# Attention values stored unturned and divided when they are reloaded, copies moved in SP's list, row blocks first in a key block

## The reference

```python
xn = layernorm(x)
q, k, v = xn @ Wq.T, xn @ Wk.T, xn @ Wv.T        # 16 query heads, 8 key heads, 16 numbers each
energy = q . k + alibi                            # alibi: -|i - j| * 2^-(head + 1)
att = softmax(energy / 4) @ v                     # two query heads share a key head
attention = att @ Wo.T + bo
scale = max(abs(xn)) / 127, per token
linear = (round(xn / scale) as int8 @ weight_q.T) * scale * weight_scale + bias
out = x + attention + linear
```

## Time and profile before

| | |
|---|---|
| median of three runs | 1607.19 us (1605.15 to 1607.93) |
| profiled execution, its span | 1606.43 us, 1604.5 us |
| PE busy | 1507.3 us, 94% |
| DVE busy | 1394.1 us, 87% |
| ACT busy | 1183.8 us, 74% |
| POOL busy | 1073.4 us, 67% |
| granted TensorE clock, mean | 0.978 |
| chain that ended last | PE 53%, DVE 31%, issue 8%, SP 4%, DMA 3% |

### The profile page before, as it was taken

One profiled execution on the slowest core, in us unless ns is written; L12 is line 12 of the kernel. 1 busy time (PEld: TensorE's weight loads), 2 busy tenths in 40 slices (PEclk: granted clock), 3 DMA queues, 4 the chain that ended last, 5 costly groups with the idle time before them and its releaser, 6 DMA issues.

```text
span 1604.5 us, 42517 instructions
## 1 busy us (share of the span) xinstructions
PE 1507.3 (94%) x16284; PEld 584.2 (36%) x16284; DVE 1394.1 (87%) x1698; ACT 1183.8 (74%) x2331; POOL 1073.4 (67%) x1627
## 2 busy tenths in 40 slices
PE   5789989999899998999989999899998999899999
PEld 5323323333333333333333334333333333233333
DVE  6889989999799997999979999799987988899991
ACT  3467777777687775887757887677776777688885
POOL 6457877777688875787757787577785776433332
PEclk9899999999999999999999999999999999999999
DMA  6423233343324333333333333333333332212211
GB/s 169 130 62 84 71 99 79 89 98 84 105 72 106 96 79 98 93 93 101 84 84 95 103 90 90 89 94 97 94 86 85 95 85 69 80 44 70 70 42 61
DMA packets 197291, 140.98 MB, mean 88 GB/s; under 512 B 107040, under 2 KB 165728, under 8 KB 197088
## 3 DMA queue, kind: packets, MB, share of 16 engines
q1 hardware_dynamic: 197088, 138.27, 33.0%
HBM read 81.40 MB, written 35.63 MB: 73 GB/s over the span
## 4 chain that ended last, share of the span: by engine, by line
PE 53%; DVE 31%; issue 8%; SPq 4%; DMA 3%; POOL 0%; ACT 0%; POOLq 0%; ACTq 0%
DVE row_max L999 29%; PE ps_ring L1279 17%; PE ps_pv L1355 15%; PE ps_row L1296 11%; PE ps_ring L1395 4%; PE ps_ring L1415 3%; DMA q_again<-q 2%; PE ps_ring L1398 1%; DVE pv_turned L1039 1%; PE ps_row L1279 1%; PE ps_ring L1409 1%; SPq L497 1%; PE ps_row L1387 1%; SPq L464 0%; DMA base<-x 0%
## 5 line engine op out<-in xcount | busy, mean ns | idle before, releaser
L999 DVE TENSOR_REDUCE row_max<-ps_row 128x1 f32<-128x1024 f32 x1024 | 1199.2, 1213 | 153.8 <-PE ps_row L1298 138.5
L1171 ACT ACTIVATE probs<-ps_ring 128x512 f32<-128x512 f32 x2048 | 1083.7, 601 | 284.8 <-PE ps_ring L1279 282.3
L1279 PE MATMUL ps_ring<-q,k 122*32 122x512 bf16 x8192 | 639.2, 385 | 5.6 <-DMA q<-neg_max_t 4.7
L762 POOL TENSOR_TENSOR probs<-probs,near 128x256 f32<-128x256 f32 x512 | 374.2, 731 | 368.5 <-ACT probs L1171 362.8
L1355 PE MATMUL ps_pv<-probs,v_unit 128*32 128x512 f32 x4096 | 537.9, 601 | 0.0
L1279 PEld LDWEIGHTS ps_ring<-q,k 122*32 122x32 bf16 x8192 | 216.5, 95 | 511.7 <-ACT probs L1171 324.6
L1296 PE MATMUL ps_row<-k,q 64*128 64x512 bf16 x944 | 329.7, 390 | 68.1 <-DMA q_again<-q 43.2
L1298 PE MATMUL ps_row<-k_again,q_again 64*128 64x512 bf16 x944 | 329.6, 390 | 0.0
L1296 PEld LDWEIGHTS ps_row<-k,q 64*128 64x128 bf16 x944 | 83.9, 93 | 362.9 <-issue 197.8
L1355 PEld LDWEIGHTS ps_pv<-probs,v_unit 128*32 128x32 f32 x4096 | 125.2, 110 | 55.1 <-issue 9.1
L1298 PEld LDWEIGHTS ps_row<-k_again,q_again 64*128 64x128 bf16 x944 | 83.8, 93 | 0.0
(11 more groups left out here) (84 smaller groups left out, 1009.1 us busy)
## 6 DMA issues: line engine op xcount, KB each, us to landing
parts_dram<-parts SPq DMA_DIRECT2D x59, 288.0 KB, 3.3
q_again<-q SPq DMA_DIRECT2D x63, 256.0 KB, 3.4
token_b<-token_dram SPq DMA_DIRECT2D x53, 256.0 KB, 4.0
q<-parts_dram SPq DMA_DIRECT2D x128, 96.0 KB
k<-parts_dram SPq DMA_DIRECT2D x256, 32.0 KB
q<-parts_dram SPq DMA_DIRECT2D x128, 64.0 KB
att_dram<-att_unit SPq DMA_DIRECT2D x126, 64.0 KB
att_t<-att_dram SPq DMA_DIRECT2D x56, 128.0 KB, 2.9
```

What stands on the lines that cost most here:

```text
L762: pool.tensor_tensor(here, here, near[:, u % KV_HEADS, :].rearrange("p (e n) -> p e n", e=GROUP), ALU.mult).then_inc(weighted, 1)
L999: dve.tensor_reduce(row_max[:, par, e, qb:qb + 1], ps_row[qb % 2][:, :], AX_X, ALU.max, negate=True).then_inc(row_max_found, 1)
L1171: act.activation(probs[:, c % PBUFS, e, h * HALF:(h + 1) * HALF], ring_bank(u, c, e, h), ACT.Exp, scale=SCALE).then_inc(ring_freed, 1)
L1279: mm = pe.matmul(to[at, :], weights[:, at], moving, start=start, stop=stop)
```

## The change

1. **Values unturned.** DVE's two transposes, its reciprocal of the turned sums and the multiplication by it (on DVE or POOL) go, but for the last unit. ACT copies `ps_pv` to `att_raw` after the exponentials of c = 1 (`keep_pv`). SP stores all 128 rows (`store_att`), reads the rows of sums back as 128 by 16 (`load_sums`), DVE takes the reciprocal before the fourteenth reduction of the unit (`find_rsum`, in c = 6), and SP stores it (`store_rsum`). When a pair of tiles is loaded, its reciprocals come along, each row repeated 16 times (`load_att_r`), and POOL multiplies both in c = 0 of the odd unit (`share`).
2. **SP's list.** The copies of a late set are issued near the front of the next unit's list. The store of the values stands ahead of the set's loads, and the load of the sums behind them. The store of the reciprocals stands behind `place_max` and ahead of a late set's loads. All row blocks now use the copies; `row_block` is left for the start alone, with 64 rows of the operands. So the first set's 64 rows are loaded first, and `place_max` of unit 0 stands ahead of one pair of copies.
3. **PE's list.** The two row blocks stand first in a key block, and `qkv_whole` ahead of `outputs`.
4. **End.** The last batch's values are multiplied by DVE (`share_last`), the first half in c = 3 of unit 62; all eight projections of the second half come after the last `pv_block`.

```diff
         for c in range(BLOCKS):
             items = [(u, c, e, h) for e in range(GROUP) for h in range(2)]
             if c == 1:
+                items += [(u, "qkv", t % PAIR) for t in f["made"]]
                 items += [(u, "outputs", t % PAIR) for t in f["proj"] or f["made"]]
-                items += [(u, "qkv", t % PAIR) for t in f["made"]]
...
             def store_att(u):
 
-                wait(sp, att_unit_ready, u + 1)
...
+                sp.wait_ge(pv_read, u + 1)
+                sp.dma_start(att_dram[u // KV_HEADS, u % KV_HEADS].rearrange("e h r n -> (e h r) n"),
+                             att_raw[:, u % 2, :]).then_inc(att_stored[u % 2], 16)
+
+            def load_sums(u):
+
+                sp.wait_ge(att_stored[u % 2], 16 * (u // 2 + 1))
+                wait(sp, rsum_ready, u - 1)
+                sp.dma_start(sums[:, u % 2, :],
+                             att_dram[u // KV_HEADS, u % KV_HEADS, :, :, HEAD_DIM, :].rearrange(
+                                 "e h (k n) -> (e h) k n", n=SUMS)).then_inc(sums_loaded[u % 2], 16)
+
+            def store_rsum(u):
+
+                sp.wait_ge(rsum_ready, u + 1)
+                sp.dma_start(rsum_dram[u // KV_HEADS, u % KV_HEADS].rearrange(
+                    "e (k n) -> (e k) n", n=SUMS), rsum[:, u % 2, :]).then_inc(rsum_stored[u % 2], 16)
...
             load_set(2, 2)
+            load_again(1, 1)
...
-            load_again(1, 1)
+            place_max(0, 0)
             load_again(2, 2)
-            place_max(0, 0)
 
             def unit(u, f):
                 if f["next_x"]:
                     next_x(u + X_AHEAD)
                 if f["xt"]:
                     load_xt(u + 2 + PREP_AHEAD)
+                if u + 2 < UNITS and late_set(u + 2):
+                    load_again(u + 2, (u + 2) % SETS)
+                if f["prev"]:
+                    store_att(u - 1)
                 if f["row_set"] and not late_set(u + 3):
                     next_set(u + 3)
-                if u % PAIR == 1:
-                    store_att(u - 1)
                 for t in f["normed"]:
                     store_token(t)
...
+                if f["prev"]:
+                    load_sums(u - 1)
...
                 for t in f["made"]:
                     store_parts(t, t % 2)
...
                 if f["token"]:
                     load_token(u + 1 + PREP_AHEAD)
                 if not f["last"]:
                     place_max(u + 1, (u + 1) % SETS)
-                if f["prev"] and u % PAIR == 0:
-                    store_att(u - 1)
-                for t in f["next_att"]:
-                    load_att_t(t, t % 2)
+                for t in f["next_att"][:1]:
+                    load_att_t(t)
+                if f["prev"] and not f["last"]:
+                    store_rsum(u - 1)
                 if f["row_set"]:
                     if late_set(u + 3):
                         next_set(u + 3)
                     else:
                         load_again(u + 3, (u + 3) % SETS)
-                if u + 2 < UNITS and late_set(u + 2):
-                    load_again(u + 2, (u + 2) % SETS)
+                for t in f["next_att"][:1]:
+                    load_att_r(t)
                 for t in finished(u):
                     store_out(t, t % 2)
...
+            def share(t):
+
+                pool.wait_ge(att_t_loaded, 16 * 2 * EC * (t // PAIR + 1))
+                pool.tensor_tensor(att_t[:, :, :], att_t[:, :, :], att_r[:, :, :],
+                                   ALU.mult).then_inc(att_t_ready, 1)
...
             def find_rsum(u):
 
-                dve.wait_ge(pv_read, u + 1)
-                wait(dve, norm_done, u)
...
+                dve.wait_ge(sums_loaded[u % 2], 16 * (u // 2 + 1))
+                wait(dve, rsum_stored[u % 2], 16 * (u // 2))
+                dve.reciprocal(rsum[:, u % 2, :], sums[:, u % 2, :]).then_inc(rsum_ready, 1)
...
+                        if i == 13 and f["prev"]:
+                            find_rsum(u - 1)
                         if i < BLOCKS and f["row_heads"] >= 1:
                             reduce_block(u + 1, (u + 1) % 2, 1, i)
                         if i >= BLOCKS and f["row_heads"] >= 2:
                             reduce_block(u + 2, u % 2, 0, i - BLOCKS)
...
+            def keep_pv(u):
+
+                act.wait_ge(pv_done, BLOCKS * (u + 1))
+                wait(act, att_stored[u % 2], 16 * (u // 2))
+                act.activation(att_raw[:, u % 2, :], ps_pv[:, :], ACT.Copy).then_inc(pv_read, 1)
...
                     if i == BLOCKS:
                         wait_row_set(u + 2, (u + 2) % SETS)
-                        if not late_set(u + 2):
-                            wait_again(u + 2)
-                    if late_set(u + 2):
-                        row_block(u + 2, (u + 2) % SETS, 0, i - BLOCKS)
-                    else:
-                        half_row_block(u + 2, (u + 2) % SETS, 0, i - BLOCKS)
+                        wait_again(u + 2)
+                    half_row_block(u + 2, (u + 2) % SETS, 0, i - BLOCKS)
...
             def unit(u, f):
                 for c in range(BLOCKS):
+                    ahead_row_block(u, f, 2 * c)
+                    ahead_row_block(u, f, 2 * c + 1)
                     if c == 0:
                         pe.wait_ge(set_loaded[u % SETS], set_count(u, u % SETS, WHOLE_SET))
                     col_half(u, c, 0, 0)
                     col_half(u, c, 0, 1)
-                    ahead_row_block(u, f, 2 * c)
-                    ahead_row_block(u, f, 2 * c + 1)
                     col_half(u, c, 1, 0)
```

More of the change, by code:

```diff
@@ L92 @@
 ALIBI_LOADS = 2
-FIRST_ROWS = K_LOADS + Q_LOADS + ALIBI_LOADS
+NEAR_PAIRS = tuple(pair for pair in PAIRS if pair[0] < ROW_K)
+FAR_PAIRS = tuple(pair for pair in PAIRS if pair[0] >= ROW_K)
+FIRST_ROWS = 2 * len(NEAR_PAIRS) + ALIBI_LOADS
 def made_unit(t):
@@ L190, in build @@
 def build(nc, x, x_t, wqk_t, wv_t, wo_t, wo_last_t, w8_t, w_scale, bias_attn, bias_lin, q_alibi, k_alibi, diag,
[L191 removed]
+          eye, parts_dram, token_dram, att_dram, rsum_dram, out):
     ctx = ExitStack()
@@ L454, in load_set, with rows @@
                 g, tok = u % KV_HEADS, (u // KV_HEADS) * SEQ
-                def rows(dst, chunk, row, pick, loaded=set_loaded[slot]):
-                    for at, q_parts, k_parts in PAIRS:
+                def rows(dst, chunk, row, pick, pairs=PAIRS, loaded=set_loaded[slot]):
+                    for at, q_parts, k_parts in pairs:
                         use = q_parts if pick == "q" else k_parts
@@ L473, in rows @@
                                              src.rearrange("d j n -> (d j) n")).then_inc(loaded, 16)
[L475 to L480, removed]
+                chunk, row = g // (KV_HEADS // 2), g % (KV_HEADS // 2) * GROUP * HEAD_DIM
+                if u == 0:
+                    rows(k_set[:, slot, :], QK_CHUNKS - 1, 0, "k", NEAR_PAIRS, first_rows_loaded)
+                    rows(q_set[:, slot, 0, :], chunk, row, "q", NEAR_PAIRS, first_rows_loaded)
+                    rows(q_set[:, slot, 1, :], chunk, row + HEAD_DIM, "q", NEAR_PAIRS)
+                    rows(k_set[:, slot, :], QK_CHUNKS - 1, 0, "k", FAR_PAIRS)
+                    for e in range(GROUP):
+                        rows(q_set[:, slot, e, :], chunk, row + e * HEAD_DIM, "q", FAR_PAIRS)
+                else:
+                    rows(k_set[:, slot, :], QK_CHUNKS - 1, g * HEAD_DIM, "k")
+                    for e in range(GROUP):
+                        rows(q_set[:, slot, e, :], chunk, row + e * HEAD_DIM, "q")
                 if u >= SETS - 1:
@@ new lines, in wait_units, with heads_of, load_att_t @@
+            def wait_units(stored, units):
+                for i in range(2):
+                    sp.wait_ge(stored[i], 16 * len(range(i, units, 2)))
+            def heads_of(c):
+                return slice(c * (KV_HEADS // EC), (c + 1) * (KV_HEADS // EC))
+            def load_att_t(t):
+                b, half, at = t // BLOCKS, t % BLOCKS // (BLOCKS // 2), t % (BLOCKS // 2) * P
+                wait_units(att_stored, (b + 1) * KV_HEADS)
+                if t >= PAIR:
+                    wait_filled(sp, projected_unit(t - PAIR), "outputs", 1)
+                for c in range(EC):
+                    sp.dma_start(att_t[:, c, :],
+                                 att_dram[b, heads_of(c), :, half, 0:HEAD_DIM, at:at + PAIR * P].rearrange(
+                                     "g e d n -> (g e) d n")).then_inc(att_t_loaded, 16)
@@ L892, in unit @@
                                 add_weighted(made)
-                    if c == 3 and f["prev"] and u % PAIR == 0:
-                        norm(u - 1)
+                    if c == 0:
+                        for t in f["proj"][:1]:
+                            share(t)
                     if c == 1:
@@ L1203, in unit @@
                             exps(u, c, e, h)
+                    if c == 1 and f["prev"]:
+                        keep_pv(u - 1)
                     if c == 1:
```

(4 more changed lines are left out.)

174 lines of the change are left out of this document (82 added, 92 removed).

## The result

The changed kernel takes 1665.14 us, the median of four runs (1654.69 to 1666.81), against 1607.56 (1605.15 to 1608.81): a ratio of 1.035, 95% interval 1.031 to 1.039. It is slower by 3.5%, where 1562 us was forecast. The profiled execution is the fastest of the four: 1654.69 us, a span of 1652.9, 48.4 us above the one before. So the profile holds 48.4 of the 57.6 us; the other three have a mean granted clock of 0.961 to 0.963, against 0.967 in it.

The account below looks back on a forecast made before the run. PE and DVE holding each other in plain stretches, plus late sets. Terms -45 + 4.8 - 15.2 + 9.5 + 1.6 - 2.5 + 1.5 = -45.3 us from 1606.43: about 1562 us, 8-in-10 range 1539 to 1592.

Parts of the forecast that it names:

- The step that failed: Loads on SP's queue land 2.2 us after issue; used for late sets' last load and for the sums.
- Late sets: 59.0 us from late sets goes; copies needed in c = 4 leave 14 (chain: 1.2 us wait); term -45 us.
- Sums: In even units DVE's reciprocal waits 0.2 us for sums read back through DRAM; term 4.8 us (0 to 41).
- The first rival: DVE waits for sums in every even unit, 31 us per us of landing above 2.2; 1615 us, chance 0.11.
- The two rivals: Sums late in even units (1615 us, chance 0.11); late sets' copies still late in c = 4 (1583 us, 0.15).
- The argument from small pieces: Sums go in 64-byte pieces, under a 512-byte bound, so might land at 3.9 us; some 36 us worse.
- DVE: Even units' 0.49 us of old values work goes, -15.2 us; new reciprocal costs 0.15 us in 63 units, +9.5.
- Order on PE: Row blocks first in a key block only turn a cycle; cost 0 in plain stretches.
- Start: Row blocks of c = 0 fill PE's wait for `place_max` of unit 0; -2.5 us (-4 to 0).
- POOL: POOL's `share` in c = 0 of the odd unit is hidden before the projection needs it; cost 0.
- the cover that the prediction named: `qkv_whole`, ahead of the projection at the end of c = 1, hides POOL's `share`; cost 0.
- End: DVE multiplies 1,024 columns in c = 3 of unit 62 and PE's projection waits: +1.5 us; moved projections 0.

Follow-up runs that it names:

- e4: The kernel before, with only the late sets' copies moved to the front of the next unit's list and all row blocks made with copies: 1569.18 us, ratio 0.976.
- e2: The changed kernel with the sums and reciprocals as 16 partitions by 128 numbers, in pieces of 512 bytes instead of 64: 1720.4 us, ratio 1.070.
- e1: The changed kernel with DVE's reciprocal of an even unit moved from before its fourteenth reduction to behind its sixteenth: 1601.78 us, ratio 0.996.
- e3: The changed kernel with the load of the sums issued behind the set's five loads of keys, not behind the whole set: 1597.61 us, ratio 0.993.
- e6: e5 with PE's new order, the two row blocks first in a key block: 1552.48 us, ratio 0.966.
- e8: e6 with 64 rows of the operands in the first pass's row blocks, in place of 120: 1562.45 us, ratio 0.972.
- e9: The changed kernel with sums loaded mid-set, late sets' first rows first, copies right behind the set, both ahead of the reciprocals' store: 1574.08 us, ratio 0.980.
- e5: e4 with a late set's first 64 rows loaded first, and its copies issued right behind the set, waiting for those loads alone: 1554.24 us, ratio 0.967.

## Why the prediction was wrong

**The step that failed** is one duration, used in two terms: 2.2 us for a load to land. It was read from two issues of `att_t`. Both loads that mattered stand behind or at the end of a whole set and land 4.1 to 4.2 us after their issue. The kernel before could have told. Over its whole span `att_t` takes 2.9 us, and `token_b`, a larger load that stands right behind the set in even units, takes 4.0; the last load of its own sets took 4.2:

```profile
token_b<-token_dram SPq DMA_DIRECT2D x53, 256.0 KB, 4.0
att_t<-att_dram SPq DMA_DIRECT2D x56, 128.0 KB, 2.9
```

**Late sets.** Term -45, measured -9.8. With the old list and order the time was nearly that of the term (e4: 38.9 us saved), though the sets landed as late there: the copies had more time. The changed kernel needs the copies earlier, by the moved row blocks and the store ahead of the set, which the prediction had counted. Set the landing to 4.2 in its chain and the wait of 1.2 us becomes 3.2; measured 3.7, and then, after six of the seven waits, the lower clock, which it had not counted at all.

**Sums.** Term +4.8. The load left 1.5 us ahead of its slot and not 2.2, since the set took 8.3 us to issue (475.78 to 484.07) and not 7.5, and it landed 1.9 us later than taken. The first rival's price (31 us for each us, so 58 at 4.07) came close: +56.3 us in the other units. In part that is luck: their 23 waits are 44.6 us, and the slow matmuls after six of them, some 1.7 us each, were not in the price. Its total, 1615 us, did not, because it kept the late sets' saving. The two rivals had the same cause and came together; they had been given chances as if one excluded the other. The argument from small pieces, for which the Trainium skill's rule was cited (DMA: Bandwidth & Descriptors, Why small descriptors are slow (HBM only)), gave the right landing for a wrong reason: pieces of 512 bytes land no earlier (e2).

**DVE.** -15.2 + 9.5 is -0.18 us for a pair. e1 shows 46.09 against 46.25, but there the even units' reciprocal stands elsewhere. With the reciprocals in their places and no wait a plain pair takes 46.20 us (e3), and 46.13 with the new order on PE and the old values (e6). So the new order gave 0.12 us, put at nothing, and the new values gave nothing in a plain pair, put at 0.18: a miss, though a small one. 54.5 us less work on DVE bought no time there, since it lay beside waiting.

**Order on PE:** put at nothing; no difference that the times can tell (e6). **Start:** -2.5 forecast, +0.1 measured. The order alone gives it (e6: the turn for unit 3 at 134.31, against 136.85). The 64 rows, which the prediction gave no price, take it back: the changed kernel's clock is 0.50 from 35 to 80 us too, and its first turn comes 30.2 us after its first row block, against 22.1 before, as in e8. **POOL:** 0.8 us in the changed kernel, but 8.0 in e9, where the cover that the prediction named is missing and no other wait hides it. **End:** right.

**What is left of the change.** With the sums' landing mended and the late sets' in part it is at 1574 to 1576 us, still 12 to 14 above the forecast; the kernel before with such late sets is at 1552 to 1554. So the late copies are the gain, and the rest of the change costs some 22 us. Plain pairs in the middle of the span hardly show it (46.19 us in e9, 46.13 in e6): it lies in the late pairs, the last eight units and the end, as e9 has them. How much of it is the new way of the values alone was not tested.

**Open:** why the three loads of `L485` took 2.32 us to issue there and 1.34 in most other units; whether the waits for `place_max` are why e9's late pairs stay above e6's by about 1 us; why the clock rises in e9's first pass and not in e8's; and e8's 3 us at the start. Not tried: the copies ahead of a late set's far rows.

## What to carry to other kernels

Take a landing from a load that stands at the same place of the same queue, or from the wait for the transfers around it; the size of the pieces said nothing here, the thirteen loads ahead added some 2 us (e3 and the units without a set). Where one duration feeds several terms, its error moves them together, so let the rivals share it too. A load that is needed soon goes into the middle of a burst of loads that are not, and half a set can be waited for by itself (e5); what is then issued behind the other half lands late in its turn.

## What the runs showed of the hardware

- In the changed kernel's even units, where PE stood idle behind the wait for the sums, the granted clock fell after none of the 18 idle times under 1.9 us and after 7 of the 12 from 2.0 to 3.1 us, for about a key block; in the five of these 7 in the middle of the span the wait then cost 1.5 to 1.9 us more.
- With 64 rows of the operands in the first pass the granted clock stayed at 0.50 (1.2 of 2.4 GHz) from 45 to 80 us, with PE busy in all of it (e8); with 120 rows it was 1.00 from 43 to 70 us (e6). From the first row block to the first turn it took 30.2 us, against 22.3. Of the seven profiled kernels with 64 rows, six stayed at 0.50 past 80 us; in e9 the clock rose at 61 us.
- DVE's reciprocal goes by the numbers in a partition: 0.26 us for 128 x 16, 0.94 us for 16 x 128, the same count of numbers.
